# Moving ACT's copy of the attention output bank two exponentials later in an AdaLN transformer kernel

## Chip, core and metric

The kernel runs on one NeuronCore of a Trainium2 chip (trn2). The metric is the device time of one execution in microseconds; times are medians of several runs. The engines are PE (TensorE, matrix products, with PEld its weight loads), DVE (VectorE), ACT (ScalarE), POOL (GpSimd) and SP (SyncE, which issues DMAs). PSUM has eight banks of 128 x 512 fp32 values; PE writes them, ACT and DVE read them.

## What is computed

Two AdaLN blocks on x of shape (8, 512, 128). The change lies in the attention of the first block; the rest (a routed feed-forward layer, a state-space layer, a second routed layer) is as it was.

```python
h = _layernorm(x) * (1 + ca) + sa                 # per batch modulation
q, k, v, o = x @ W.T + b + 2 * (x @ A.T @ B.T)    # each a linear layer with a rank-8 addition
# 16 heads of width 8 over 512 tokens, softmax attention
x = x + ga * o(softmax(q k^T / sqrt(8)) v)
h = _layernorm(x) * (1 + cb) + sb
x = x + gb * moe(h)                               # 8 experts, top 2, plus a shared one
# then block 2: selective state space layer, second MoE layer
```

## The kernel before

The program has five stages; `attention()` (stage 1) is followed by `ffn0` and three more. Each engine runs a program of its own, written out in one function per engine (`pe`, `dve`, `act`, `pool`, `sp`), and they meet by semaphores: `k.wait_ge(name, key)` waits until that key was signalled, `k.inc(name, key)` signals. The order on an engine is the order of the code; no scheduler moves anything.

**Units and steps.** Attention works on NB = 8 batches of 64 units each, a unit being one head and one tile of 128 keys against 512 queries. All engines' loops run over b and over the step i = 0, 2, ..., 62, each step holding units i and i + 1. Sixteen units, four heads by four key tiles, are a *group*; a batch has four groups, g = 0 to 3.

**PE, per step** (lines 1121 to 1157): the scores of unit i (`expu`, L1042: matmul of K and Q with 51 rows) into a bank; `maxima` (L1026), which computes scores for the row maxima of units that come 46 units later (LEAD); the scores of unit i + 1; and at i mod 4 = 2 `pv(n // 4 - 1)` (L1053), eight matmul passes that multiply V with the exponentials of four units and accumulate over the four key tiles of a group. So the last pv of a group stands at steps 18, 34, 50 and at step 2 of the next batch, and the first pv of the next group at 22, 38, 54 and 6. Other work stands at single steps: `zt` (transposes for hT, L997) at 4, `ho(b, g)` (transposes of the copied output, L997) at 24, 40, 56 and 8, `mxt` (transposes of the maxima's parts, L1020) at 22 and 54, `qk` (projection, L1008) at 28 and 36, `vp` at 44, `features` (L1076) and `route` (L417) at 40 and 48.

**Banks.** Scores for ACT go round banks 4, 5 and 6 (`bank_a`): a new use waits for the reader of the use three before it, so the scores of unit n wait for the exponential of unit n - 3. Maxima, `ho` and some others go round two pairs of banks (`bank_d`). All pv results go to one bank, PVB = 7: pv of key tile 0 overwrites it and therefore waits for the copy of the group before (`ov`, lines 1050 and 1051):

```python
if kt == 0 and m:
    k.wait_ge("ov", m // 4 - 1)
```

**ACT, per step** (lines 838 to 867): `exp` (L790) of units i and i + 1, reading the score bank and writing E. Then, at single steps, `ht` (L760, scale and shift into hT) at 4, `otr` (L813) at 12, `rows` (L783, the tile nms) at 22 and 54, `qk` (L768, the tile qf) at 28 and 36, `v` (L776) at 44, `features` (L802, hTf) and `logits` (L806) at 40 and 48 (34 and 38 in the last batch), and `ovc(b, g)` (L796): it waits for the group's last pv and copies bank 7 into ov. `ovc` stands at steps 18, 34 and 50 for groups 0 to 2, and at step 2 of the next batch for group 3; the very last one is behind the loop. A copy takes 0.60 us.

**DVE** reduces each pair of maxima banks (L878, about 1.22 us), turns ov's transposes into otok (`otk`, L886 and L890), adds the result to X (`xo`, L896) and computes layer norm statistics (L245). In batches 4 and 6, and once in 7, it also does the routing of the next layer in small steps (L370 to L499). **POOL** splits q and k into parts (L641 to L647), normalises, splits the maxima (`max_parts`, L658 to L666), splits expert weights (L697 to L700) and in batches 5 to 7 issues scatters, each four of them held back until ACT has done a given exponential (`paced`). POOL's splits wait for qf. The maxima's parts go on to `mxt` on PE, to `rows` on ACT and by DMA into Q.

Of the kernel before, what the change touches and what calls it, by code (L numbers as in the profile page):

```python
# [131 lines left out]
def adaln_kernel(nc, x_d, p0_d, p1_d, p2_d, p3_d, w12_d, small_d, ones_d, rows_d, out_d):  # L132
    ctx = ExitStack()
    with ctx:
# [285 lines left out]
        def act_exp(e, k, g):  # L420
            L, w, a, c = group(g)
            k.wait_ge("lgx", g)
            e.activation(L, L, ACT.Exp)
            e.activation(w[:, 4, :, 3], w[:, 4, :, 3], ACT.Exp).then_inc(*k.inc("pw", g))
# [89 lines left out]
        def attention():  # L514
# [239 lines left out]
            def act(e, k):  # L754
                def ht(b):
                    k.wait_ge("mf", 0, 5)
                    k.wait_ge("zt_mm", b)
                    if b:
                        k.wait_ge("v_mm", b - 1)
                    e.activation(hT[:], PS[:, bank["hT", b], :], ACT.Identity, bias=mf[:, 0, 0, b:b + 1],  # L760
                                 scale=mf[:, 0, 1, b:b + 1]).then_inc(*k.inc("hT", b))

                def qk(b, i):
                    k.wait_ge("qk_mm", b, i)
                    k.wait_ge("bqs")
                    if b:
                        k.wait_ge(*spl(i, b - 1))
                    e.activation(qf[:, i], PS[:, bank["qf", b, i], :], ACT.Identity, bias=bqs[:, i:i + 1],  # L768
                                 scale=(SC, 1.0)[i]).then_inc(*k.inc("qf", b, i))

                def v(b):
                    k.wait_ge("v_mm", b)
                    k.wait_ge("const", "v")
                    if b >= 3:
                        k.wait_ge("pv_mm", 16 * (b - 3) + 15)
                    e.activation(V[:, b % 3, :, :, 0:8], PS[:, bank["v_ok", b], :].rearrange("p (t h d) -> p t h d", t=4, h=16),  # L776
                                 ACT.Copy).then_inc(*k.inc("v_ok", b))

                def rows(b, hf):
                    k.wait_ge("mxt_mm", b, hf)  # L780
                    if b:
                        k.wait_ge(f"dmx{hf}", b - 1)
                    e.activation(nms[:, hf], PS[0:24, bank["nms", b, hf], :], ACT.Copy).then_inc(*k.inc("nms", b, hf))  # L783

                def exp(n):
                    m = n // 4
                    k.wait_ge("exp_mm", n)
                    if m >= 4:
                        k.wait_ge("pv_mm", m - 4)
                    e.activation(E[:, m % 4, n % 4], PS[:, bank["exp", n], :], ACT.Exp).then_inc(*k.inc("exp", n))  # L790

                def ovc(b, g):
                    k.wait_ge("pv_mm", 16 * b + 4 * g + 3)
                    if 4 * b + g >= 2:
                        k.wait_ge("ho_mm", 4 * b + g - 2)
                    e.activation(ov[:, g % 2], PS[:, PVB, :], ACT.Copy).then_inc(*k.inc("ov", 4 * b + g))  # L796

                def features(b):
                    k.wait_ge("ht_mm", b)
                    if b:  # L800
                        k.wait_ge("rt_mm", b - 1)
                    e.activation(hTf[:], PS[:, bank["hTf", b], :], ACT.Copy).then_inc(*k.inc("hTf", b))  # L802

                def logits(b):
                    k.wait_ge("rt_mm", b)
                    e.activation(lg[:, 4 * b:4 * b + 4, :].rearrange("p t e -> p (t e)"), PS[:, bank["lgt", b], 0:32],  # L806
                                 ACT.Copy).then_inc(*k.inc("lgt", b))

                def otr(b):
                    k.wait_ge("ot_mm", b)  # L810
                    if b:
                        k.wait_ge("op_mm", b - 1)
                    e.activation(oT[:], PS[:, bank["oT", b], :], ACT.Copy).then_inc(*k.inc("oT", b))  # L813
# [24 lines left out]
                for b in range(NB):  # L838
                    for i in range(0, 64, 2):
                        exp(64 * b + i)  # L840
                        exp(64 * b + i + 1)
                        if b + 2 < NB and i == 4:
                            ht(b + 2)
                        if b:
                            if i == 2:
                                ovc(b - 1, 3)
                            if i == 12:
                                otr(b - 1)
                        if i == 22:
                            rows(b, 1)  # L850
                        if b + 2 < NB:
                            if i in (28, 36):
                                qk(b + 2, (i - 28) // 8)
                            if i == 44:
                                v(b + 2)
                        if i in (18, 34, 50):
                            ovc(b, i // 16 - 1)
                        if b and i == (40 if b < NB - 1 else 34):
                            features(b - 1)
                        if b and i == (48 if b < NB - 1 else 38):  # L860
                            logits(b - 1)
                        if b in (4, 6) and i == 38:
                            act_exp(e, k, b // 2 - 2)
                        if b == NB - 1 and i == 46:
                            act_exp(e, k, 2)
                        if b + 1 < NB and i == 54:
                            rows(b + 1, 0)
# [103 lines left out]
            def pe(e, k):  # L971
# [189 lines left out]
                op(NB - 1)  # L1161

            return pe, dve, act, pool, sp

        parts_a = attention()
# [1394 lines left out]
```

## Time and profile before

| | |
|---|---|
| median of 3 runs | 995.49 us (995.11 to 996.27) |
| profiled execution, its own time | 995.49 us |
| profiled execution, span | 993.7 us |
| attention stage in it | about 60 to 487 us |
| busy: PE | 843.4 us (85%) |
| busy: DVE | 743.4 us (75%) |
| busy: ACT | 631.8 us (64%) |
| busy: POOL | 499.8 us (50%) |
| L790, 512 exponentials | 274.3 us busy, mean 600 ns |
| L796, 32 copies of bank 7 | 19.1 us busy, mean 597 ns |
| L878, 256 maxima | 307.0 us busy, mean 1221 ns |

The page divides the span into busy time per engine, gives the chain of work that ended last, and groups instructions by line. A timeline gives instructions one after another in order of time, neighbours of the same kind merged; in brackets behind a row stands how long the engine was idle before it and who released it. In a table of stretches, each engine's busy time is followed by the number of its instructions, and PEclk is the granted TensorE clock as a share of the full 2.4 GHz.

### The profile page before, as it was taken

The numbers are of one execution on the slowest core, as the hardware profiler recorded it, in microseconds if no ns is written. First come the engines' busy times: TensorE is split into PE (matmuls) and PEld (weight loads), VectorE is DVE, ScalarE is ACT, GpSimd is POOL, SyncE is SP. The second block draws the span as 40 slices with busy tenths as digits, with TensorE's granted clock in tenths as the row PEclk, the third lists the DMA queues.
The fourth block names the chain that finished last, engine by engine and source line by source line (L and its number), as shares of the span: only waits on it lengthen the run. The fifth ranks groups of instructions, "written<-read, shape, count | busy, mean of one in ns | idle before, by whom it ended". The sixth has DMA issues, their size and how long they took to land.

```text
span 993.7 us, 14183 instructions
## 1 busy us (share of the span) xinstructions
PE 843.4 (85%) x4630; PEld 464.0 (47%) x4630; DVE 743.4 (75%) x1562; ACT 631.8 (64%) x1111; POOL 499.8 (50%) x794
## 2 busy tenths in 40 slices
PE   5499999999988989897896999999937469978886
PEld 4232222323222222221475877777734257757774
DVE  5588888888898869883386788978759568966771
ACT  2138888888876867577484777776626726554662
POOL 3703463737365656346353078766766055752211
PEclk9559999999999989798598999999957779988997
DMA  6834636464636364202115266766260000000000
GB/s 199 187 105 134 160 123 159 130 152 136 146 121 162 109 176 114 78 23 109 56 33 182 65 241 218 247 209 240 85 237 14 19 1 1 0 1 11 22 22 32
DMA packets 45077, 110.78 MB, mean 111 GB/s; under 512 B 7806, under 2 KB 20606, under 8 KB 39494
## 3 DMA queue, kind: packets, MB, share of 16 engines
q1 hardware_dynamic: 39436, 98.33, 33.1%
q0 software_dynamic: 4992, 10.36, 3.0%
q10 hardware_dynamic: 576, 1.19, 0.4%
q8 instruction: 37, 0.61, 0.3%
q14 instruction: 36, 0.29, 0.1%
HBM read 57.65 MB, written 51.03 MB: 109 GB/s over the span
## 4 chain that ended last, share of the span: by engine, by line
PE 46%; DVE 18%; POOL 15%; issue 10%; ACT 8%; DMA 3%; SPq 1%; POOLq 0%; DVEq 0%; ACTq 0%
PE PS L1053 10%; POOL yd L1258 9%; PE PS L1042 7%; DVE mx L878 6%; PE PS L1026 5%; ACT E L790 3%; PE PS L319 2%; PE PS L321 2%; PE PS L320 2%; PE PS L997 1%; PE PS L1008 1%; ACT ov L796 1%; PE PS L1063 1%; PE PS L2385 1%; PE PS L2388 1%
## 5 line engine op out<-in xcount | busy, mean ns | idle before, releaser
L878 DVE TENSOR_REDUCE mx<-PS 128x2 f32<-128x1024 f32 x256 | 307.0, 1221 | 65.4 <-PE PS L1026 64.1
L790 ACT ACTIVATE E<-PS 128x512 f32<-128x512 f32 x512 | 274.3, 600 | 67.4 <-PE PS L1042 64.9
L1042 PE MATMUL PS<-Q,K 51*128 51x512 bf16 x512 | 166.9, 399 | 12.8 <-ACT E L790 9.7
L1026 PE MATMUL PS<-K,Q 48*128 48x512 bf16 x512 | 142.1, 414 | 29.1 <-DVE mx L878 17.3
L1053 PE MATMUL PS<-E,V 128*9 128x512 f32 x1024 | 141.1, 625 | 0.0
L1258 POOL DMA_INDIRECT yd<-yt,goes x92 | 98.1, 1066 | 42.3 <-issue 23.4
L1042 PEld LDWEIGHTS PS<-Q,K 51*128 51x128 bf16 x512 | 37.4, 95 | 164.9 <-ACT E L790 100.5
L510 POOL DMA_INDIRECT xs<-HT,pos x64 | 63.9, 999 | 79.7 <-ACT E L790 46.5
L1422 DVE TENSOR_TENSOR Gl<-Gf,Gh 128x512 fp32r<-128x512 f32 x117 | 86.0, 749 | 23.4 <-ACT Gh L1293 21.0
L1287 ACT ACTIVATE Gf<-PS,WR 128x512 f32<-128x512 f32 x92 | 63.4, 689 | 39.1 <-PE PS L321 38.3
L2296 DVE SCALAR_TENSOR_TENSOR cb<-ye,gt,cb 128x128 f32<-128x128 f32 x224 | 65.5, 365 | 0.0
L658 POOL CAST mh<-mx 128x32 bf16<-128x32 f32 x16 | 3.4, 211 | 109.4 <-DVE mx L878 109.1
L2179 ACT ACTIVATE ye<-PS 128x1024 f32<-128x1024 f32 x32 | 32.7, 1023 | 37.1 <-PE PS L2388 37.1
L1026 PEld LDWEIGHTS PS<-K,Q 48*128 48x128 bf16 x512 | 29.2, 95 | 55.9 <-DVE mx L878 34.9
L1417 DVE CAST Gh<-Gf 128x512 fp32r<-128x512 f32 x62 | 28.5, 460 | 17.2 <-ACT Gf L1287 17.2
L1293 ACT ACTIVATE Gh<-Gf 128x512 fp32r<-128x512 f32 x62 | 39.2, 632 | 2.0
L319 PE MATMUL PS<-Hh,WR 128*128 128x512 f32 x92 | 40.4, 439 | 0.0
L321 PE MATMUL PS<-Gl,WR 128*128 128x512 f32 x92 | 36.4, 395 | 0.0
L321 PE MATMUL PS<-Hl,WR 128*128 128x512 f32 x92 | 36.3, 395 | 0.0
L320 PE MATMUL PS<-Hh,WR 128*128 128x512 f32 x92 | 36.3, 394 | 0.0
L319 PE MATMUL PS<-Gh,WR 128*128 128x512 f32 x92 | 36.2, 394 | 0.0
L320 PE MATMUL PS<-Gh,WR 128*128 128x512 f32 x92 | 36.2, 393 | 0.0
(415 smaller groups left out, 1881.6 us busy)
## 6 DMA issues: line engine op xcount, KB each, us to landing
WR<-wsd SPq DMA_DIRECT2D x23, 1028.0 KB, 5.2
xs<-zero SPq DMA_DIRECT2D x8, 2112.0 KB, 7.5
wsd<-wsp SPq DMA_DIRECT2D x8, 1024.0 KB, 4.1
Q<-dqk SPq DMA_DIRECT2D x16, 384.0 KB, 6.0
K<-dqk SPq DMA_DIRECT2D x16, 384.0 KB, 8.9
HT<-xs SPq DMA_DIRECT2D x23, 264.0 KB, 4.6
dqk<-SPL SPq DMA_DIRECT2D x31, 192.0 KB, 2.8
stage<-in_w SPq DMA_DIRECT2D x9, 516.0 KB, 5.3
```

The costliest lines, as they stand in the source:

```text
L319: e.matmul(o, wh, xh, start=start, stop=False)
L320: e.matmul(o, wl, xh, start=False, stop=False)
L321: return e.matmul(o, wh, xl, start=False, stop=stop)
L510: e.indirect_dma_start(out=xs[:, :], out_offset=bass.IndirectOffsetOnAxis(ap=pos[:, x, i:i + 1], axis=0), in_=HT[:, i, :], in_offset=None) ...
L790: e.activation(E[:, m % 4, n % 4], PS[:, bank["exp", n], :], ACT.Exp).then_inc(*k.inc("exp", n))
L878: e.tensor_reduce(mx[:, 2 * s % 96:2 * s % 96 + 2], PS[:, o:o + 2, :], AX.X, ALU.max, negate=True).then_inc(*k.inc("max", s))
L1026: return e.matmul(PS[:, o + n % 2, :], Q[r, b % 3, h // 2, qt * P:(qt + 1) * P], K[r, b % 3, h // 2, :], start=True, stop=True)
L1042: e.matmul(PS[:, o, :], K[r, b % 3, h // 2, kt * P:(kt + 1) * P], Q[r, b % 3, h // 2, :], start=True, stop=True).then_inc(*k.inc("exp_mm", n))
L1053: p = e.matmul(PS[32 * j:32 * j + 9, PVB, :], V[:, b % 3, kt, 4 * g + j, :], E[:, m % 4, j, :], start=(kt == 0), stop=(kt == 3))
L1258: e.indirect_dma_start(out=yd[:, :], out_offset=bass.IndirectOffsetOnAxis(ap=goes[:, n % 8, t:t + 1], axis=0), in_=yt[:, n % 2, t * P:(t + ...
L1422: e.tensor_tensor(Gl[:, u % 8], Gf[:, u % 3], Gh[:, u % 8].bitcast(F32), ALU.subtract).then_inc(*k.inc("gl", u))
L2296: m = e.scalar_tensor_tensor(o, y, g, o, ALU.mult, ALU.add)
```

## The change

Two conditions in ACT's program change: the copy of group 3 of the batch before moves from step 2 to step 4, those of groups 0 to 2 move from steps 18, 34 and 50 to 20, 36 and 52. No other engine's program changes.

```diff
--- before.py
+++ after.py
@@ -842,7 +842,7 @@
                         if b + 2 < NB and i == 4:
                             ht(b + 2)
                         if b:
-                            if i == 2:
+                            if i == 4:
                                 ovc(b - 1, 3)
                             if i == 12:
                                 otr(b - 1)
@@ -853,7 +853,7 @@
                                 qk(b + 2, (i - 28) // 8)
                             if i == 44:
                                 v(b + 2)
-                        if i in (18, 34, 50):
+                        if i in (20, 36, 52):
                             ovc(b, i // 16 - 1)
                         if b and i == (40 if b < NB - 1 else 34):
                             features(b - 1)
```

Within a step the code's order holds: at step 4 the copy stands behind `ht`, at step 36 behind `qk`.

ACT's program at the end of batch 3 and the start of batch 4, first before, then with the change (E is an exponential, lg the logits, ov the copy, nms the rows of maxima, hT the modulated input; xN is a run of N):

```order
L806 ACTIVATE lg<-PS 128x32
L790 ACTIVATE E<-PS 128x512 x2
L796 ACTIVATE ov<-PS 128x512
L790 ACTIVATE E<-PS 128x512 x4
L783 ACTIVATE nms<-PS 24x512
L790 ACTIVATE E<-PS 128x512 x12
L796 ACTIVATE ov<-PS 128x512
L790 ACTIVATE E<-PS 128x512 x2
L760 ACTIVATE hT<-PS,mf 128x512
L790 ACTIVATE E<-PS 128x512 x8
```

```order
L806 ACTIVATE lg<-PS 128x32
L790 ACTIVATE E<-PS 128x512 x4
L796 ACTIVATE ov<-PS 128x512
L790 ACTIVATE E<-PS 128x512 x2
L783 ACTIVATE nms<-PS 24x512
L790 ACTIVATE E<-PS 128x512 x14
L760 ACTIVATE hT<-PS,mf 128x512
L796 ACTIVATE ov<-PS 128x512
L790 ACTIVATE E<-PS 128x512 x8
```

Both copies moved behind two more exponentials, and the second one also behind hT.

ACT's program in the middle of batch 4, around steps 28 to 38, before and with the change (qf is the copy of a projection):

```order
L790 ACTIVATE E<-PS 128x512 x6
L768 ACTIVATE qf<-PS,bqs 128x512
L790 ACTIVATE E<-PS 128x512 x6
L796 ACTIVATE ov<-PS 128x512
L790 ACTIVATE E<-PS 128x512 x2
L768 ACTIVATE qf<-PS,bqs 128x512
L790 ACTIVATE E<-PS 128x512 x2
```

```order
L790 ACTIVATE E<-PS 128x512 x6
L768 ACTIVATE qf<-PS,bqs 128x512
L790 ACTIVATE E<-PS 128x512 x8
L768 ACTIVATE qf<-PS,bqs 128x512
L796 ACTIVATE ov<-PS 128x512
L790 ACTIVATE E<-PS 128x512 x2
```

The copy moved behind two exponentials and the second qf.

## Rows read from the trace of the kernel before

**Rows 1.** Busy time by stretches; header, then 140 to 190.
```profile
core 0: us, PE busy (x) PEld busy (x) DVE busy (x) ACT busy (x) POOL busy (x), PEclk, DMA share, GB/s
...
140.00:190.00 50.00, 48.14 (x329) 14.38 (x328) 42.76 (x47) 41.64 (x80) 27.71 (x59) 1.00 0.56 151
```

**Rows 2.** Chain of work that ended last, 200 to 330 us, shares by line.
```profile
by line: PE PS L1053 23.3%; DVE mx L878 18.4%; PE PS L1042 15.6%; PE PS L1026 10.7%; issue 5.6%; ACT E L790 4.9%; ACT ov L796 2.8%; PE PS L1008 2.4%; PE PS L997 1.8%; PE PS L417 1.5%; PE PS L1020 1.2%; DVE wk L374 1.1%; PE PS L1013 0.8%; PE
```

**Rows 3.** Timeline, batch 2, third group: start, us, engine, line, tiles, [idle <-releaser].
```profile
201.88 1.05 PE L1053 MATMUL PS<-E,V 128*9 128x512 f32 x8
...
202.86 0.39 PE L1042 MATMUL PS<-Q,K 51*128 51x512 bf16 x1
...
203.00 0.60 ACT L796 ACTIVATE ov<-PS 128x512 f32<-128x512 f32 x1
...
204.14 0.39 PE L1042 MATMUL PS<-Q,K 51*128 51x512 bf16 x1 [0.23 <-ACT E L790]
...
204.46 1.04 PE L1053 MATMUL PS<-E,V 128*9 128x512 f32 x8
...
206.62 1.22 DVE L878 TENSOR_REDUCE mx<-PS 128x2 f32<-128x1024 f32 x1 [0.76 <-PE PS L1026]
...
209.41 0.39 PE L1042 MATMUL PS<-Q,K 51*128 51x512 bf16 x1
...
209.83 2.06 ACT L790 ACTIVATE E<-PS 128x512 f32<-128x512 f32 x4 [0.70 <-PE PS L1042]
```

**Rows 4.** Timeline, a boundary at step 4 with hT.
```profile
214.15 0.39 PE L1042 MATMUL PS<-Q,K 51*128 51x512 bf16 x1
...
214.69 0.66 PE L997 MATMUL PS<-p,Z 128*128 128x128 f32 x4
...
215.73 0.79 ACT L760 ACTIVATE hT<-PS,mf 128x512 f32<-128x512 f32 x1
...
216.23 1.04 PE L1053 MATMUL PS<-E,V 128*9 128x512 f32 x8
...
217.85 1.23 DVE L878 TENSOR_REDUCE mx<-PS 128x2 f32<-128x1024 f32 x1 [0.56 <-PE PS L1026]
```

**Rows 5.** Timeline, a boundary at step 36 with qf, batch 1.
```profile
141.74 1.12 PE L1008 MATMUL PS<-hT,Wk 128*128 128x512 f32 x2
...
142.91 0.69 ACT L768 ACTIVATE qf<-PS,bqs 128x512 f32<-128x512 f32 x1
...
143.34 1.05 PE L1053 MATMUL PS<-E,V 128*9 128x512 f32 x8
...
144.96 1.22 DVE L878 TENSOR_REDUCE mx<-PS 128x2 f32<-128x1024 f32 x1 [0.29 <-PE PS L1026]
```

**Rows 6.** Timeline, longer waits of PE, held-up DVE operations.
```profile
281.98 0.39 PE L1026 MATMUL PS<-K,Q 48*128 48x512 bf16 x2 [1.43 <-DVE mx L878]
...
289.78 0.39 PE L1026 MATMUL PS<-K,Q 48*128 48x512 bf16 x2 [2.35 <-DVE mx L878]
...
299.35 1.07 DVE L452 COPY HT<-wk 128x12 f32<-128x12 f32 x1
...
363.78 1.03 PE L1020 MATMUL PS<-p,S 128*24 128x128 f32 x4 [2.73 <-POOL S L666]
...
408.46 2.34 DVE L453 TENSOR_TENSOR HT<-wk 128x8 f32<-128x8 f32 x1
...
411.98 1.11 PE L459 MATMUL PS<-wk,p 128*128 128x64 f32 x4 [2.82 <-DVE mx L878]
```

**Rows 7.** Busy time by stretches, low clock, and 254.3 at full.
```profile
363.50:371.50 8.00, 7.68 (x36) 2.08 (x39) 3.68 (x5) 3.81 (x8) 0.63 (x3) 0.57 0.99 279
254.30:259.70 5.40, 4.95 (x36) 1.55 (x32) 4.12 (x6) 3.76 (x8) 3.16 (x7) 1.00 0.49 153
305.40:309.00 3.60, 3.60 (x19) 0.65 (x19) 1.84 (x2) 2.27 (x5) 3.07 (x12) 0.53 0.69 228
411.90:422.00 10.10, 10.02 (x45) 3.88 (x46) 6.01 (x13) 4.96 (x10) 1.68 (x7) 0.52 0.23 91
```

## The prediction

> **What bounds the kernel now.** The edit touches only the attention stage (about 60 to 487 us), so after the page I asked for busy time by stretches. In 50 us of batches 1 and 2 PE is busy 48.14 us at full granted clock, DVE 42.76 and ACT 41.64 [rows 1]: PE has almost no slack, the others little. The chain of work from 200 to 330 us agrees [rows 2]: mostly PE's pv, score and maxima matmuls, DVE's maxima 18.4%, ACT's exponentials 4.9% and the ov copy 2.8%. ACT binds only where PE waits for one particular ACT result, and the copy is such a place.
>
> Third view, the timeline around one copy [rows 3]. pv of the old group ends at 202.93 (201.88 + 1.05). ACT copies bank 7 from 203.00 to 203.60. The next group's first pv starts at 204.46. The copy had been done for 0.86 us by then, so PE was not waiting for it but for its own work and, through the ring of banks, for the next exponential (0.23 us before 204.14).
>
> **The change, part by part.** Nothing is added or removed. ACT's program moves 31 of the 32 copies behind the next two exponentials; the last, after the loop, stays. PE's and DVE's programs are the same, so the next group's first pv (steps 22, 38, 54 and 6) stands where it stood, and it waits for the copy. I take three kinds of boundary.
>
> *Plain boundary* (steps 20, 52, and 4 in batches 6 and 7) [rows 3]. The matmul for the next exponential starts at 202.86. An idle ACT starts an exponential 0.42 us after such a matmul starts (209.41, 209.83), and back-to-back ones start 0.48 us apart (four in 2.06 us, 0.60 each). So exponentials at 203.28 and 203.76, the copy at 204.24 to 204.84, and pv 0.05 us later (as 204.14 follows the end of the exponential before it at 204.09): 204.89 instead of 204.46, **0.43 us late**. The exponentials come 0.21 us earlier than now, but PE's matmul behind them stands before the same pv in program order, so that gain ends in the wait. The Trainium skill (ScalarE: Activation LUTs, What ACT_TABLE_LOAD costs) has an ACTIVATE of 186 + 0.833 x 512 = 612 ns and an overlap of 93, a pitch of 0.52 us; by that the delay would be estimated at 0.50. The trace shows 0.48 for the same thing and is used.
>
> *With hT* (step 4, batches 1 to 5) [rows 4]. Here the copy now stands behind hT too. The next matmul starts at 214.15, so exponentials at 214.57 and 215.05, hT at 215.53 (its transposes end at 215.35), the copy 0.66 later (0.79 less the overlap), 216.19 to 216.79, pv at 216.84 against 216.23: **0.61 us**.
>
> *With qf* (step 36, batches 0 to 5) [rows 5]. The copy now stands behind qf, which waits for a 1.12 us projection ending at 142.86. qf keeps its start of 142.91; the copy follows at 143.49 to 144.09 and pv starts at 144.14 against 143.34: **0.80 us**.
>
> What hides it? Behind each such pv DVE is idle until PE's next maxima: 0.76 us [rows 3], 0.56 [rows 4], 0.29 [rows 5]. With DVE released by PE there, PE behind the pv and ACT fed by PE, nothing regains the time in batches 0 to 3: (0.43 + 0.80 + 0.43 + 0.61) x 4 = 9.08 us.
>
> From batch 4 on some boundaries fall in front of a stall with another anchor [rows 6], and there I count nothing. Batch 4, first boundary: PE waits 1.43 us for DVE, which is busy with routing; the third stands before a like wait; after the second, DVE's L452 takes 1.07 us for a tiny copy while POOL runs a long operation, whose start hangs on qf, which does not move. Batch 5: PE waits 2.73 us for POOL's maxima parts after the third boundary, covering second and third (0.80 + 0.43). Batch 6: a routing wait after the first, and 2.34 us of DVE behind POOL after the second. Batch 7: the same kind after the second. What remains is 0.61 (batch 4, last), 0.43 twice (batch 5, first and last), 0.25 and 0.43 (batch 6, third, partly covered, and last) and 0.43 twice (batch 7): 3.01 us. **Sum: +12.1 us.** The bounds: if all absorbed delays counted too, 4.6 more (0.43 + 0.80 + 0.49, 1.23, 0.86 + 0.18, 0.65); if none propagated, 0.
>
> *The clock.* After the 2.73 us wait the granted clock is 0.57 over 8 us, thus mostly at 1.2 GHz. 36 matmuls take 7.7 us there (8.00 less 0.28 of waiting), while the 36 of the same place in batch 3 take 5.4 at clock 1.00 [rows 7]: the low clock costs 2.3 us. The change shortens this wait, since PE arrives 1.23 us later and POOL does not: 1.50 are left. A wait of 2.35 us at 289.78 did no harm: the matmuls behind it still take 0.39 us [rows 6]. So I take it that the clock stays up: **-2.3 us**. The Trainium skill (TensorE: Matmul & The Clock Gate, Part 1) says that idling throttles PE and work restores it, between just these two levels; no row here shows the shortened wait itself.
>
> Forecast: 12.1 - 2.3 = +9.8 us on the profiled execution, whose own time is 995.49 (span 993.7 and 1.8 around it), also the median of the three runs: **1005.3 us**.
>
> **Rivals.**
> 1. The clock in batch 5 falls all the same (between 305.4 and 309 it was 0.53 [rows 7] with no long wait just before), or what one place regains another loses: 995.5 + 12.1 = 1007.6. Up to 1012.2 if the cover of batches 4 to 7 fails too, for instance because DVE's short routing steps slip behind the next long POOL operation (1.07 and 2.34 us there).
> 2. More clock is regained: in batch 4, and in batch 6, where the 2.82 us wait at 411.98 [rows 6] shrinks by up to 0.43 to 2.39, close to the 2.35 that did no harm. The low stretches are 3.6 us at 0.53 and 10.1 us at 0.52 [rows 7], so they could give back 1.7 and 4.8 us if PE alone set the pace; DVE sets part of it, I take half, 3.3: 1002.0.
> 3. Not slower: ACT absorbs a two-slot move and the time stays at 995.5. For it: ACT is idle 8 of 50 us [rows 1]. Against it: that is an average, and the copy moves by 1.24 us at a plain boundary where its reader leaves room for 0.86 less the 0.05 of PE's start. That room is the point from which it decides: were the pv bound to start at 204.89 by something else, nothing would show. The Trainium skill (Perfetto Trace Analysis, Identifying the Most-Contended Engine) says to go by the engine with the highest occupancy, which is not ACT; taken as a rule, the move would cost nothing.
> 4. Faster: the next exponential comes 0.21 us earlier, and PE waits 0.23 us for it today. If the pv found the copy done, 31 x 0.2 = 6 us would be won: 989. It decides only if the copy ended before about 204.2; by the sum it ends at 204.84.
>
> **How the numbers follow.** Forecast 0.45, rival 1 0.30 (of it 0.08 above 1010.5), rival 2 0.17, rival 3 0.05, rival 4 0.03. The range 1001.5 to 1010.5 holds the first three but for the top of rival 1. A measurement of this kernel can tell about 0.2% (2 us) from no change; only rivals 3 and 4 are not slower by that. Slower 0.92, same 0.05, faster 0.03.
>
> **What would show it.** In the profile after, the pv behind a copy starts 1.96 us after the old group's last pv ended instead of 1.53 at plain boundaries, and 0.61 and 0.80 us later than now in the other kinds; PE's idle time before it is released by the ov copy, which it is at none of these now; that copy's share of the chain rises. Batches 0 to 3 grow by 2.3 us each, the stage ends near 497 instead of 487, and all behind it is only shifted. Batch 5's wait for POOL is 1.5 us with a granted clock near 1 behind it. It would be wrong if the pv starts move by much less (my chain of 0.48s is off), if DVE's idle times don't pass the delay on (it had a backlog that I don't see), or if the granted clock falls at new places.

## The result and the profile after

The change makes the kernel slower. The kernel with the change takes 1010.64 us (median of 4 runs, 1006.30 to 1013.02) against 995.88 us for the kernel before beside it (4 runs, 995.11 to 996.58): ratio 1.0139, 95% interval 1.0109 to 1.0169. Measured again in two later sets, each on a chip of its own, the same kernel gave 1.0128 (1.0099 to 1.0156) and 1.0071 (1.0046 to 1.0097). The forecast, 1005.3, is a ratio of 1.0098; the first median lies 0.1 us above the upper end of its range, 1010.5. Three more runs on record with the first four took 1006.42, 1009.88 and 1010.96 us; the median of all seven is 1009.88, inside the range.

The page's lines that answer to the table of before. Columns of the groups: busy us, mean ns | idle us just before them, and who ended most of it.

```profile
span 1011.4 us, 14214 instructions
...
PE 846.5 (84%) x4630; PEld 463.8 (46%) x4630; DVE 740.0 (73%) x1562; ACT 631.6 (62%) x1111; POOL 497.7 (49%) x794
...
L878 DVE TENSOR_REDUCE mx<-PS 128x2 f32<-128x1024 f32 x256 | 306.8, 1221 | 82.4 <-PE PS L1026 76.5
L790 ACT ACTIVATE E<-PS 128x512 f32<-128x512 f32 x512 | 276.8, 599 | 84.3 <-PE PS L1042 81.2
...
L1053 PE MATMUL PS<-E,V 128*9 128x512 f32 x1024 | 140.1, 620 | 19.1 <-ACT ov L796 18.4
```

PE and ACT do the same work. What is new is the idle time in front of PE's pv matmuls, 19.1 us, of which 18.4 were ended by the ov copy; before it was 0.0. It stands at all 31 boundaries, 0.6 us each on average.

The wait at a plain boundary, timeline, batch 2, third group; start, duration, engine, and in brackets idle time and releaser:

```profile
209.43 1.05 PE L1053 MATMUL PS<-E,V 128*9 128x512 f32 x8
...
210.41 0.39 PE L1042 MATMUL PS<-Q,K 51*128 51x512 bf16 x1
...
210.83 1.08 ACT L790 ACTIVATE E<-PS 128x512 f32<-128x512 f32 x2 [0.43 <-PE PS L1042]
...
211.49 0.39 PE L1042 MATMUL PS<-Q,K 51*128 51x512 bf16 x1
...
211.80 0.60 ACT L796 ACTIVATE ov<-PS 128x512 f32<-128x512 f32 x1
...
212.28 1.10 ACT L790 ACTIVATE E<-PS 128x512 f32<-128x512 f32 x2
...
212.46 1.04 PE L1053 MATMUL PS<-E,V 128*9 128x512 f32 x8 [0.59 <-ACT ov L796]
...
214.62 1.23 DVE L878 TENSOR_REDUCE mx<-PS 128x2 f32<-128x1024 f32 x1 [1.22 <-PE PS L1026]
```

The old group's last pv ends at 210.48. The score matmul at 211.49 is held by the ring as before, the copy runs from 211.80 behind two exponentials, and pv starts 0.06 us after its end. From 210.48 to 212.46 are 1.98 us, against 1.53 in [rows 3]. DVE then waits 1.22 us for PE, against 0.76 there: the whole delay is passed on.

The same at step 4 behind hT, and at step 36 of batch 1 behind qf:

```profile
221.18 1.05 PE L1053 MATMUL PS<-E,V 128*9 128x512 f32 x8
...
223.55 0.78 ACT L760 ACTIVATE hT<-PS,mf 128x512 f32<-128x512 f32 x1
...
224.21 0.61 ACT L796 ACTIVATE ov<-PS 128x512 f32<-128x512 f32 x1
...
224.88 1.04 PE L1053 MATMUL PS<-E,V 128*9 128x512 f32 x8 [0.77 <-ACT ov L796]
...
226.49 1.23 DVE L878 TENSOR_REDUCE mx<-PS 128x2 f32<-128x1024 f32 x1 [1.34 <-PE PS L1026]
```

```profile
144.63 1.05 PE L1053 MATMUL PS<-E,V 128*9 128x512 f32 x8
...
146.15 1.12 PE L1008 MATMUL PS<-hT,Wk 128*128 128x512 f32 x2
...
147.31 0.69 ACT L768 ACTIVATE qf<-PS,bqs 128x512 f32<-128x512 f32 x1 [0.19 <-PE PS L1008]
...
147.90 0.59 ACT L796 ACTIVATE ov<-PS 128x512 f32<-128x512 f32 x1
...
148.54 1.04 PE L1053 MATMUL PS<-E,V 128*9 128x512 f32 x8 [0.73 <-ACT ov L796]
```

From the end of the old group's last pv (start plus duration of the first row of each) to the next group's first pv are 224.88 - 222.23 = 2.65 us and 148.54 - 145.68 = 2.86 us. Measured in the same way, the kernel before has 2.02 and 2.07 at the boundaries of [rows 4] and [rows 5].

By stretches, the first to be laid beside [rows 1]:

```profile
core 0: us, PE busy (x) PEld busy (x) DVE busy (x) ACT busy (x) POOL busy (x), PEclk, DMA share, GB/s
140.00:190.00 50.00, 45.96 (x315) 14.05 (x312) 40.36 (x44) 39.88 (x76) 25.66 (x55) 1.00 0.54 140
375.00:383.00 8.00, 7.17 (x53) 1.88 (x45) 5.71 (x8) 5.44 (x12) 1.23 (x6) 1.00 0.97 282
425.00:435.00 10.00, 9.63 (x45) 3.03 (x44) 6.12 (x13) 4.87 (x10) 1.68 (x7) 0.51 0.02 7
```

In the same 50 us PE is busy 45.96 us instead of 48.14, with 315 matmul records instead of 329: 4 to 5% less work in the same time, at full clock. The chain from 202 to 340 us, by line, answers to [rows 2]:

```profile
by line: PE PS L1053 25.2%; PE PS L1042 16.0%; DVE mx L878 14.7%; PE PS L1026 10.9%; issue 5.6%; ACT E L790 3.7%; ACT ov L796 3.0%; PE PS L1008 3.0%; PE PS L1013 2.4%; PE PS L997 2.1%; ACT hT L760 1.7%; PE PS L417 1.4%; PE PS L1020 1.2%; DV
```

I had expected the copy's share to rise, and it hardly does, 2.8% to 3.0%. It was in the chain before as well, ahead of the exponential that PE's ring waits for: its 8 rows there have 4.2 us of 138, which is 3.0%. What moved is what hangs on it, PE's pv (23.3% to 25.2%) in place of DVE's maxima (18.4% to 14.7%). The idle time of the pv group is the clearer sign.

Below I compare times from the end of one group's last pv to the end of another group's. Let P0 be the end of batch 0's first group, P16 that of batch 4's, P31 that of batch 7's last but for the copy behind the loop. The column "low" is the time between P16 and P31 in which the granted clock was at 1.2 GHz; between P0 and P16 it was at 2.4 GHz throughout, in every profile.

| profile | P0 to P16 | P16 to P31 | low | behind P31 |
|---|---|---|---|---|
| before | 195.0 | 207.4 | 37.5 | 510.3 |
| before, second profile | 195.0 | 208.2 | 33.9 | 511.2 |
| after | 204.4 | 209.7 | 34.1 | 514.7 |
| after, second profile | 204.4 | 209.3 | 37.4 | 507.7 |
| after, third profile | 204.4 | 206.5 | 23.9 | 510.8 |
| one slot | 196.9 | 206.5 | 30.7 | 506.7 |
| two slots, first | 198.6 | 208.5 | 34.1 | 510.6 |
| three slots | 212.2 | 218.9 | 47.8 | 510.5 |
| group 3 only, twice | 197.5, 197.5 | 209.3, 209.1 | 34.1, 37.5 | 510.5, 507.7 |
| groups 0 to 2 only, twice | 201.9, 201.9 | 215.8, 214.3 | 44.4, 54.6 | 510.6, 511.2 |
| parts first | 195.0 | 211.3 | 41.0 | 510.6 |
| whole change, parts first | 204.4 | 211.6 | 30.7 | 514.0 |

The first half reproduces to 0.1 us for one program, and the other two columns don't.

### The profile page after: what moved, and what is told of

Same layout as the page of the kernel before. It is cut to its first block, busy times and chain, and to the rows that moved or that the text cites. A ratio compares the mean times of both kernels' runs of the same rounds, so it can differ in the third digit from the quotient of the medians.

```text
span 1011.4 us, 14214 instructions
## 1 busy us (share of the span) xinstructions
PE 846.5 (84%) x4630; PEld 463.8 (46%) x4630; DVE 740.0 (73%) x1562; ACT 631.6 (62%) x1111; POOL 497.7 (49%) x794
## 4 chain that ended last, share of the span: by engine, by line
PE 45%; DVE 16%; POOL 15%; issue 12%; ACT 8%; DMA 3%; SPq 1%; POOLq 0%; DVEq 0%; ACTq 0%
PE PS L1053 10%; POOL yd L1258 9%; PE PS L1042 7%; DVE mx L878 6%; PE PS L1026 5%; PE PS L319 2%; ACT E L790 2%; PE PS L320 2%; PE PS L321 2%; PE PS L1008 1%; PE PS L997 1%; ACT ov L796 1%; PE PS L1063 1%; PE PS L2385 1%; PE PS L2387 1%
## 5 line engine op out<-in xcount | busy, mean ns | idle before, releaser
L1042 PE MATMUL PS<-Q,K 51*128 51x512 bf16 x512 | 167.7, 401 | 10.3 <-ACT E L790 6.9
L1026 PE MATMUL PS<-K,Q 48*128 48x512 bf16 x512 | 143.3, 416 | 30.4 <-DVE mx L878 17.7
L1053 PE MATMUL PS<-E,V 128*9 128x512 f32 x1024 | 140.1, 620 | 19.1 <-ACT ov L796 18.4
L1258 POOL DMA_INDIRECT yd<-yt,goes x92 | 96.6, 1050 | 45.1 <-issue 23.9
L1053 PEld LDWEIGHTS PS<-E,V 128*9 128x9 f32 x1024 | 15.2, 89 | 65.8 <-issue 35.4
```

What stands on the lines that cost most here:

```text
L1026: return e.matmul(PS[:, o + n % 2, :], Q[r, b % 3, h // 2, qt * P:(qt + 1) * P], K[r, b % 3, h // 2, :], start=True, stop=True)
L1042: e.matmul(PS[:, o, :], K[r, b % 3, h // 2, kt * P:(kt + 1) * P], Q[r, b % 3, h // 2, :], start=True, stop=True).then_inc(*k.inc("exp_mm", n))
L1053: p = e.matmul(PS[32 * j:32 * j + 9, PVB, :], V[:, b % 3, kt, 4 * g + j, :], E[:, m % 4, j, :], start=(kt == 0), stop=(kt == 3))
L1258: e.indirect_dma_start(out=yd[:, :], out_offset=bass.IndirectOffsetOnAxis(ap=goes[:, n % 8, t:t + 1], axis=0), in_=yt[:, n % 2, t * P:(t + ...
```

## The experiments

There are three sets of four kernels, each set on one chip and beside runs of the kernel before.

**The change again, and three other places for the copy.** The change itself:

> The changed kernel once more, to see what of its 1006.3 to 1013.0 us is its own. My theory: every pv behind a copy starts 1.98 us (plain), 2.65 (with hT) and 2.86 (with qf) after the old group's last pv ended, in this profile as in the first, and the attention stage is about 11 to 12 us longer than before; the median is 1.1 to 1.6% above before. What varies between executions is the stage behind (ffn0), which has the same instructions: it should differ by some us between the two profiles although the attention stage does not. Rival: the spread lies in the attention stage, then the distances above differ between the two profiles.

Measured: 1007.44 us (1005.85 to 1009.49) against 996.2, ratio 1.0128 (1.0099 to 1.0156). The distances from the old group's last pv to the new group's first are 1.98, 2.65 and 2.86 in batches 0 to 3, as in the first profile. P0 to P31 is 11.3 us longer than before, and the part behind it 7.0 us shorter than in the first profile, with the same instructions.

One slot: the copy between the two exponentials, at the steps of the change (the old places are gone here and in the next two).

```diff
                         exp(64 * b + i)
+                        if b and i == 4:
+                            ovc(b - 1, 3)
+                        if i in (20, 36, 52):
+                            ovc(b, i // 16 - 1)
                         exp(64 * b + i + 1)
```

> The copy stands behind one exponential instead of none (between the two units of steps 20, 36, 52 and 4). My theory, the room of 0.86 us before the waiting pv: plain boundaries have the copy from P + 0.83 to P + 1.43, pv starts at P + 1.51 against 1.53 now, so nothing is lost. With hT and with qf a third bank user stands between, the scores of the second unit after it wait for the exponential that the copy now pushes back, to P + 1.91, and pv comes at P + 2.28 instead of 2.01 and P + 2.27 instead of 2.07: 0.27 + 0.20 = about 0.45 us per batch, in all about +2 us, 0.2%. Rival (each slot costs the same, about half of what two slots cost): +5 to 7 us. Rival 4 of the prediction (the earlier exponential is worth 0.2 us each time): -3 to -6 us.

Measured: 995.28 us, ratio 1.0004 (0.9983 to 1.0025); distances 1.50 (plain) and 2.30 (hT and qf), P0 to P16 +1.9 us. A plain boundary, timeline, batch 2, third group:

```profile
203.85 1.05 PE L1053 MATMUL PS<-E,V 128*9 128x512 f32 x8
...
205.75 0.59 ACT L796 ACTIVATE ov<-PS 128x512 f32<-128x512 f32 x1
...
206.22 1.10 ACT L790 ACTIVATE E<-PS 128x512 f32<-128x512 f32 x2
...
206.39 0.62 PE L1053 MATMUL PS<-E,V 128*9 128x512 f32 x4
```

The copy ends at 206.34, pv starts at 206.39 (its row holds four of the eight matmuls), 1.49 after the old pv's end at 204.90. One exponential ahead of the copy just fits into the room; that pv starts 0.03 us earlier than in before. At boundaries with qf and hT 0.24 and 0.29 us are lost, as expected, and not by pv waiting for the copy: the projection or the transposes use a score bank too, so the score matmul ahead of that pv waits for the exponential that the copy pushed back. At the qf boundary of batch 1 this exponential ends at 144.47, the matmul starts at 144.53 and pv at 144.84.

Two slots, but ahead of hT and qf:

```diff
                         exp(64 * b + i)
                         exp(64 * b + i + 1)
+                        if b and i == 4:
+                            ovc(b - 1, 3)
+                        if i in (20, 36, 52):
+                            ovc(b, i // 16 - 1)
```

> As the changed kernel, two exponentials later, but at step 4 the copy stands ahead of hT and at step 36 ahead of qf. My theory: plain boundaries as in the changed kernel, P + 1.98; the other two kinds lose nothing, since their pv is held by PE's own extra work until P + 2.0 and the copy is done at P + 1.93. So 0.86 us per batch instead of 2.27, in all about +5.8 us; less if the clock of batch 5 stays up, whose wait for POOL is then about 2.3 us. Rival (what counts is that the copy moves, not what stands ahead of it): as the changed kernel, +1.4%.

Measured: 1001.52 us, ratio 1.0064 (1.0039 to 1.0089); distances 1.98 (plain), 1.98 (hT), 2.06 (qf); P0 to P16 +3.6 us. At the hT and qf boundaries there was already slack of that size: before stood at 2.02 and 2.07. So the extra of the two mixed boundaries comes from hT and qf being ahead of the copy, not from the two exponentials.

Three slots: as one slot, but at steps 6, 22, 38 and 54.

```diff
                         exp(64 * b + i)
+                        if b and i == 6:
+                            ovc(b - 1, 3)
+                        if i in (22, 38, 54):
+                            ovc(b, i // 16 - 1)
                         exp(64 * b + i + 1)
```

> The copy one more exponential later (between the units of steps 22, 38, 54 and 6; behind hT and qf as in the changed kernel). My theory: 0.48 us more at each boundary, pv at P + 2.46 plain, 3.13 with hT, 3.34 with qf; 4.2 us per batch in batches 0 to 3, in all +20 to +26 us with what the waits of batches 4 to 7 cover. Rival (the cost of the change is one of order, once paid, for instance a lost overlap): about as the changed kernel, +10 to +14 us.

Measured: 1023.76 us, ratio 1.0285 (1.0249 to 1.0322); distances 2.47, 3.13 and 3.35, P0 to P16 +17.2 us. The first half is as expected (4.3 us per batch for 4.2), the whole is not: 28 us instead of 20 to 26, since P16 to P31 took 11.5 us more, with 47.8 us of low clock in it. The pv group of the one-slot, two-slot and three-slot kernels, idle time behind the second bar:

```profile
L1053 PE MATMUL PS<-E,V 128*9 128x512 f32 x1024 | 140.6, 622 | 2.0
...
L1053 PE MATMUL PS<-E,V 128*9 128x512 f32 x1024 | 140.9, 623 | 11.7 <-ACT ov L796 11.1
...
L1053 PE MATMUL PS<-E,V 128*9 128x512 f32 x1024 | 143.6, 635 | 34.7 <-ACT ov L796 34.7
```

The copy ended none of it with one slot, 11.1 us with two and 34.7 with three, against 18.4 with the change. At plain boundaries the distance runs 1.53, 1.50, 1.98, 2.47 for zero, one, two and three exponentials ahead of the copy: nothing for the first exponential ahead of the copy, then 0.48 for each. A copy that ACT could absorb (rival 3) would show no such step, and rival 4 wanted shorter distances than 1.53; the only gain, 0.03 us, is that of one slot.

**The two conditions apart, and the order of POOL's work.** A second profile of the kernel before:

> The kernel before once more, for a second profile. All offsets are taken against one profile of it; if that one is typical, the times from the first group's last pv to the last group's agree within 1 us (402.4 us), every pv behind a copy starts 1.53, 2.02 or 2.07 us after the old group's last pv, and batch 5's wait for POOL is 2.7 us with a low clock behind it. The stage behind attention may differ by some us (510.3 us in the first profile, 506.7 to 514.7 in the others so far); if it is always 510 here, the change has made that stage unsteady, which my theory does not explain.

Measured: 999.44 us against 1000.2, ratio 0.9998 (0.9974 to 1.0022). P0 to P31 agrees within 0.8 us and the distances of batches 0 to 3 are the same. Its batch 5 is not that of [rows 6]: the wait for POOL is 1.00 us instead of the 2.7 expected, the clock is up, and the distance at the third boundary is 3.23 us instead of 1.52; see the clock and the pause below.

Group 3 alone (`i == 2` to `i == 4`):

> One part alone: only the copy at step 2 moves to step 4, behind hT; the others stay at 18, 34, 50. My theory (delays add, each boundary by itself): 0.63 us at each of the five boundaries with hT and 0.46 at the two in batches 6 and 7, nothing at the others: +4 us, 0.4%. Rival (a boundary delay is partly regained at the next one when that one is untouched, so the parts are less than the whole): +1 to +2 us.

Measured: 1002.03 us, ratio 1.0016 (0.9992 to 1.0039). Groups 0 to 2 alone (steps 18, 34, 50 to 20, 36, 52):

> The other part alone: the copies at 18, 34, 50 move to 20, 36, 52, the one at step 2 stays. My theory: 0.46 + 0.79 + 0.46 = 1.71 us in each of batches 0 to 3, about 0.9 more from the first boundary of batch 5 and those of batch 7, about 1.4 in batch 6, less 2.3 for the clock in batch 5, whose wait for POOL is 1.5 us: +7 us, 0.7%. Together with the other part this must give the whole change, 1.3%. Rival: as for the other part, less than that.

Measured: 1013.38 us, ratio 1.0131 (1.0095 to 1.0167). Between P0 and P16 the first adds 2.53 us and the second 6.85, together the 9.38 of the whole, with the predicted boundaries touched and no other. In the times they don't share like that: the one is measured at nothing that is clear of the noise (+4 us were expected), the other at the whole, 1.3% (+7 us were expected).

POOL's parts for batch 6 ahead of the split of expert weights, so that PE finds them at step 22's `mxt` without waiting:

```diff
+                    if b == 5:
+                        max_parts(b + 1, 0)
                     wsplit(b + 1)
...
-                    if b + 1 < NB:
+                    if b + 1 < NB and b != 5:
                         max_parts(b + 1, 0)
```

> The kernel before, with one reorder on POOL in batch 5: the maxima's parts for batch 6 stand ahead of the split of an expert's weights instead of behind it. It tests the clock term. My theory: PE no longer waits 2.73 us for POOL in batch 5 and the granted clock stays at 1 behind that place: 2.7 + 2.3 = 5 us less, 0.5% faster than before. Rival (the low clock there has another cause than the wait): only the wait goes, -2.7 us, and mxt still takes 1.03 us. Second rival (the time is given back at the next place where DVE or POOL is late, batch 6's routing): -1 us or less.

Measured: 998.63 us, ratio 0.9977 (0.9952 to 1.0002). PE's rows where it used to wait, and the stretch (line numbers are two higher in this kernel: L1055 is pv, L1022 `mxt`):

```profile
364.08 1.68 PE L1055 MATMUL PS<-E,V 128*9 128x512 f32 x8
365.70 1.03 PE L1022 MATMUL PS<-p,S 128*24 128x128 f32 x4
...
364.00:367.50 3.50, 3.50 (x17) 0.66 (x16) 1.59 (x2) 1.92 (x5) 2.51 (x2) 0.55 0.18 75
```

The wait in front of the matmul of S is gone, and the clock is low all the same: pv takes 1.68 us instead of 1.05 and PEclk is 0.55 over 3.5 us. The expected gain of some 5 us did not come. The ratio would allow the rival's 2.7 us, but 1 is in its interval, and in the profile P16 to P31 is 3.9 us longer than in the first of before.

**Third set: do the parts add, and what if the wait is gone under the change?** The whole change, group 3 alone, groups 0 to 2 alone:

> The whole change once more, beside its two parts on one chip. Theory (fixed delays of 0.45, 0.63 and 0.80 us a boundary, uncovered ones only, and a clock in batches 4 to 7 that differs from execution to execution): ratio 1.012 to 1.014; P0 to P16 (from the end of batch 0's first group's last pv to batch 4's) 204.4 us, +9.4; P16 to P31 2 to 8 us more than the 207.4 of before, depending on the low clock.

Measured: 1008.95 us against 1001.92, ratio 1.0071 (1.0046 to 1.0097), below the 1.012 to 1.014 expected. P0 to P16 is the expected 204.4, but P16 to P31 is 0.9 us less than the 207.4 of before instead of 2 to 8 more, with 23.9 us of low clock for 37.5.

> Only group 3's copy moved (step 2 to 4). It was +0.16% with an interval of -0.1 to +0.4 while its profile had +4.4 us in attention. Theory: 2.5 us in batches 0 to 3, exactly, and 1 to 2 in batches 4 to 7: ratio 1.003 to 1.005. Rival: a delay of group 3 alone is regained behind the stage or by the clock, then the ratio is 1.000 to 1.002 again.

Measured: 1000.09 us, ratio 0.9988 (0.9969 to 1.0007).

> Only the copies of groups 0 to 2 moved. It was +1.31%, as much as the whole change, while its profile had +6.85 us in batches 0 to 3. Theory of fixed delays: 6.9 + about 2 = ratio 1.008 to 1.010, below the whole change by 0.3 to 0.5%. Rival: the two parts don't add, since without group 3's delay the clock in batches 4 to 7 is low for longer (44.4 us in its first profile against 34 to 37 with the whole change): ratio 1.012 to 1.014 again, and over 40 us of low clock there.

Measured: 1010.17 us, ratio 1.0083 (1.0059 to 1.0107). Group 3 alone costs nothing that can be measured for the second time, though its 2.5 us in batches 0 to 3 are there again; 0.9988 is below its expectation, and the rival's 1.000 is inside its interval. Within this set the two parts add to the whole, -0.12% and 0.83% to 0.71%, each known to about 0.25%. The mean of group 3's two ratios is 1.0002, that of groups 0 to 2 1.0107, that of the whole change's three measurements 1.0113. So the parts add within the noise, but do not seem to be in proportion to their delays. Groups 0 to 2 alone spend 44 and 55 us at low clock in P16 to P31, where the whole change spends 24 to 37, and their P16 to P31 is 5 to 9 us longer than that of the whole change, which has all their delays and more. That is the half of the rival that came true, over 40 us of low clock. Its ratio, 1.012 to 1.014 again, did not: 1.0083 is what the fixed delays gave. Where group 3's 4.2 to 4.4 us of attention time go in runs that were not profiled stays open.

> The whole change, and POOL's maxima parts for batch 6 ahead of the split of weights in the loop of batch 5, so that the wait of PE for POOL there is gone. Theory: the cover of batch 5's second and third boundary is gone with the wait, so their 0.80 and 0.43 now count: against the kernel with the parts ahead alone +1.2 us more than the whole change costs against before in batches 4 to 7, as far as the clock doesn't differ; d at the three boundaries of batch 5 as at plain and qf ones (1.98, 2.86). Time: parts ahead alone were 0.9977, so 0.9977 + 0.013 + 0.001 = 1.012. Rival: the wait was what the change regains its time from (2.3 us of clock), then 1.014 or more.

Measured: 1012.82 us, ratio 1.0107 (1.0075 to 1.0140). The clock at batch 5's place stayed up here, and P16 to P31 is 211.6 us, as with the parts ahead alone (211.3). The distances at batch 5's first and second boundary are those expected, 1.98 and 2.86. At the third it is 3.08 instead of 1.98, and with the parts ahead alone it is 3.23: the pause shown below falls there in both profiles, and the delay of this boundary does not come on top of it. The 0.80 us of the second boundary are there and still no 1.2 us appear in the sum; the low clock, 30.7 us against 41.0, differs by more than that.

## Where the prediction was right and where not

**The boundaries: right.** Predicted distances 1.96, 2.62 and 2.87 (1.53, 2.02, 2.07 and the delays), measured 1.98, 2.65 and 2.86. The step of 0.42 us from a score matmul to its exponential and 0.48 from one exponential to the next holds: the pair of exponentials starts at 210.83, 0.42 behind its matmul at 210.41, so the copy was due at 210.83 + 2 x 0.48 = 211.79, and it starts at 211.80. The three-slot kernel confirms the step a second time.

**The passing on: right.** DVE's idle time behind the pv grew by the delay, 0.76 to 1.22, and P0 to P16 by 9.4 us where the sum has 9.08. The difference is 0.02 us for each of 16 boundaries.

**The covered boundaries: partly.** Per batch I compare the increments between the ends of groups in batches 4 to 7 with the first profile of before (three profiles of after):

| | predicted | after | second | third |
|---|---|---|---|---|
| batch 4 | 0.61 | 0.78 | 0.52 | 0.88 |
| batch 5, clock in it | 0.86 - 2.3 = -1.44 | -0.75 | -1.41 | -0.77 |
| batch 6 | 0.68 | 1.89 | 1.78 | -1.24 |
| batch 7 | 0.86 | 0.36 | 0.98 | 0.20 |

Here a batch runs from the end of its first group's last pv to that of the next batch, batch 7 to P31. Batches 4, 5 and 7 are within about 0.7 us of their terms. The mis-sized term is batch 6: 0.25 and 0.43 us for two boundaries, measured 1.9, 1.8 and -1.2. The sum held the durations of PE's matmuls fixed, and they are not. PE of after in batch 6:

```profile
414.05 1.89 PE L1053 MATMUL PS<-E,V 128*9 128x512 f32 x8 [0.37 <-ACT ov L796]
...
423.35 0.66 PE L459 MATMUL PS<-wk,p 128*128 128x64 f32 x4 [0.76 <-DVE mx L878]
...
427.58 1.90 PE L1053 MATMUL PS<-E,V 128*9 128x512 f32 x8
...
431.68 1.89 PE L1053 MATMUL PS<-E,V 128*9 128x512 f32 x8 [0.37 <-ACT ov L796]
```

Here PEclk is 0.51 from 425 to 435 us, and two pv take 1.90 and 1.89 us where before has 1.90 (416.85) and 1.52 (420.50). The wait in front of L459 had fallen from 2.82 us to 0.76, far below the 2.35 that I had taken as harmless, and the clock was low for 17 us instead of 10 in this batch (6.8 from 412, 10.2 from 425). In the third profile it was low for 6.8 us there, and the same term is negative, though the wait in front of L459 was as short (0.96 us). So in the three profiles of the change this term goes with the clock. That the clock alone sets it is not shown: the second profile of before also had it low for only 6.8 us in batch 6, and that batch took 0.1 us more than in the first.

**The clock in batch 5: the outcome as predicted, the reason not shown.** Rival 1 had the clock fall all the same. In all three profiles of the change it stayed up, and the wait was 0.38, 1.48 and 0.26 us, where 1.50 was predicted. Only the 1.48 is the predicted wait; in the profiles with 0.38 and 0.26 PE was late for another reason too, the pause shown in the last section, so there the outcome is partly luck. But the step "it is the 2.73 us wait that lowers the clock" rests on one profile. Over all 14 profiles, the wait in front of that `mxt` and the clock around it:

| wait | clock there | profiles |
|---|---|---|
| 2.73, 2.68, 2.44 | low | before, one slot, two slots first |
| 1.48, 1.00, 0.48, 0.38, 0.26 | up | after (three), before again, three slots |
| 0.70 | low for 10.2 us | group 3 only, second |
| none | low | parts first, group 3 only, groups 0 to 2 only (twice) |
| none | up | whole change, parts first |

Busy time by stretches there, PEclk behind POOL's column, for the second profile of after, the second of group 3 only and the whole change with parts first; and the timeline row of the `mxt` in the first of the three:

```profile
375.00:383.00 8.00, 6.69 (x47) 1.97 (x47) 5.41 (x7) 5.07 (x10) 1.09 (x5) 1.00 1.00 291
...
366.00:376.00 10.00, 9.30 (x44) 2.27 (x40) 4.13 (x6) 5.00 (x10) 2.08 (x8) 0.51 0.85 240
...
375.00:383.00 8.00, 6.83 (x50) 1.96 (x47) 5.48 (x7) 5.09 (x11) 1.10 (x2) 1.00 0.83 256
...
375.86 0.61 PE L1020 MATMUL PS<-p,S 128*24 128x128 f32 x4 [1.48 <-POOL S L666]
```

A long wait was followed by a low clock 3 times in 3. Without one it was low 5 times in 11, and in each of these five the low stretch began ahead of the `mxt` (1.1 to 2.5 us ahead; in parts first from 364.4, before the 365.70 above), so the long wait is not the only thing that comes before it. One candidate is on record: all five have the pause that is shown in the last section, at `route` in the same batch, and the low stretch began 3.0 to 3.8 us behind the start of ACT's late copy. The four other profiles with the pause kept the clock up, and the two with neither the pause nor a long wait did as well. No run changed the pause alone, so this stays a candidate. The Trainium skill (TensorE: Matmul & The Clock Gate, Part 1) has idling lower the clock; the 3 agree with it, the 5 are not explained by a wait in front of this `mxt`. The -2.3 us is thus right against the profile on which it was based and not a property of the change: before itself had it up in its second profile.

**The upper end of the range: missed by 0.1 us by the first median.** The first profile of after is 17.7 us longer than that of before: 1.6 up to P0, 11.7 in P0 to P31 (forecast 9.8), and 4.4 behind P31, in stages whose instructions are the same. "All behind it is only shifted" is the step that did not hold: the part behind P31 took 506.7 to 514.7 us over the 14 profiles, without order by kernel; after alone had 514.7, 507.7 and 510.8. In its other two profiles the span is 1004.0 and 1003.9, 10.3 and 10.2 us above that of before, close to the 9.8. The three ratios, 1.0139, 1.0128 and 1.0071, lie on both sides of 1.0098. The range had bounds for the covers and the clock in this stage and none for the rest of the program.

**The rivals.** Not slower and faster (3 and 4) fall with the dose series. The Trainium skill (Perfetto Trace Analysis, Identifying the Most-Contended Engine) says to optimize first the engine with the highest occupancy, and to judge TensorE not by its matmuls' busy time but by the FLOPs it reaches and its weight loads (46% busy here; by these DVE, at 73%, would come first). It does not say that a move on another engine is free; read as such a rule, as rival 3 did, it fails here: 18.4 us of PE's idle time were ended by a copy on an engine that is 62% busy. Rival 2, more clock regained, is what the third profile shows (23.9 us low instead of 37.5, ratio 1.0071), and rival 1's ratio, 1007.6 / 995.49 = 1.0122, is near the 1.0128 of the second measurement, but its reason, a fallen clock in batch 5, was seen in none of the three.

**A better kernel.** None was found. The one-slot kernel is at 1.0004 and parts first at 0.9977 with 1 in its interval. The place that the copy had before is as good as any tried, and the 0.03 us that one slot wins at a plain boundary would give 16 x 0.03 = 0.5 us over the boundaries at steps 20 and 52.

## What to carry to other kernels

An operation on an engine with time to spare is free only up to the room that its own reader leaves: here 0.86 us between the copy's end and the pv that waits for it, and each further exponential of 0.48 us ahead of the copy costs 0.48 us at every plain boundary. So look for the reader's row and measure the gap before moving the writer, and count what else stands in the new place (hT, qf), since that adds to the chain. Bound the sum by the spread of a second profile of the same program too: the stretches in which the clock or a pause comes and goes moved by several us here with no edit at all.

## What was not expected of the hardware

**A pause that comes and goes.** In batch 5 there is, in some profiles, a pause around the router's matmul L417 (`route`, step 48), at the third boundary. Second profile of the kernel before, timeline:

```profile
356.97 1.06 PE L417 MATMUL PS<-p,hTf 128*128 128x8 f32 x8
...
359.37 0.20 ACT L806 ACTIVATE lg<-PS 128x32 f32<-128x32 f32 x1 [1.44 <-PE PS L417]
...
360.79 3.49 DVE L878 TENSOR_REDUCE mx<-PS 128x2 f32<-128x1024 f32 x3 [2.39 <-PE PS L1026]
...
361.48 0.39 PE L1042 MATMUL PS<-Q,K 51*128 51x512 bf16 x1 [0.98 <-ACT E L790]
...
364.82 0.61 PE L1020 MATMUL PS<-p,S 128*24 128x128 f32 x4 [1.00 <-POOL S L666]
```

L417 ends at 358.03 by the record, ACT's copy of its result starts 1.34 us later, DVE and PE follow late, and the wait for POOL is 1.00 us instead of 2.73. In the first profile of before the copy follows at 357.00, 0.04 us after L417's recorded end. ACT waits 1.35 to 2.08 us there in 9 of 14 profiles: in none of the four kernels measured first together, in all eight of the other two sets, in the first profile of after and not in the first of before. So it seems to go with the chip or the occasion rather than the kernel. In the same 9 profiles the distance at batch 5's third boundary is 3.08 to 3.34 us, where the other five have 1.50 to 2.47 by kernel. What causes the pause no record shows.

**The clock.** Its low stretches in batches 4 to 7 differ between two executions of one program (37.5 and 33.9 us; 34.1, 37.4 and 23.9; 44.4 and 54.6), with a wait of 2.35 us in front of full clock in one profile [rows 6] and none in front of a low one in another. In batches 0 to 3 it was never low; PE's waits there are at most 0.41 us before and 0.77 with the change.
